# Experts' down product as three rounded products, with the down weights split block by block

## The reference, cut to what matters

```python
gu = jnp.einsum('th,eih->eti', x2, w_gate_up)
g, u = jnp.split(gu, 2, axis=-1)
act = jax.nn.silu(g) * u
out_e = jnp.einsum('eti,ehi->eth', act, w_down)      # the down product
moe_out = jnp.einsum('eth,te->th', out_e, combine)
```

## Time and profile before

| | |
|---|---|
| median of 3 runs | 1449.4 us |
| profiled execution, its own time | 1447.74 us |
| its span | 1445.7 us |
| granted TensorE clock, mean | 0.996 |
| busy share: PE (matmul) / VectorE / ScalarE / GpSimd | 98% / 59% / 35% / 25% |

### The profile page before, as it was taken

How to read it: one execution, slowest core, us unless ns; L and a number is a source line. 1 busy time by engine, 2 the same in 40 slices (tenths; PEclk the granted TensorE clock), 3 DMA queues, 4 the chain that set the end, 5 groups by cost and what they waited for, 6 DMA issues and landing times.

```text
span 1445.7 us, 26892 instructions
## 1 busy us (share of the span) xinstructions
PE 1412.5 (98%) x9085; PEld 1126.2 (78%) x9086; DVE 846.3 (59%) x1804; ACT 512.1 (35%) x1113; POOL 361.5 (25%) x376
## 2 busy tenths in 40 slices
PE   6999997999999999999999999999999999999999
PEld 5888885777878787777878787777877788777777
DVE  5444445666666565666666565666678746243358
ACT  4333343334333333333333333334334330222242
POOL 1222223121111212121121212121112101266746
PEclk9999999999999999999999999999999999999999
DMA  6543431111111111111111101111113243654557
GB/s 223 163 131 123 132 114 43 37 41 37 34 39 38 41 29 49 36 35 37 41 40 31 49 29 41 37 41 37 48 59 102 84 169 132 223 170 161 163 172 276
DMA packets 89882, 125.95 MB, mean 87 GB/s; under 512 B 7120, under 2 KB 56272, under 8 KB 89296
## 3 DMA queue, kind: packets, MB, share of 16 engines
q1 hardware_dynamic: 82288, 100.23, 21.5%
q0 software_dynamic: 7520, 24.65, 5.2%
HBM read 87.36 MB, written 37.49 MB: 86 GB/s over the span
## 4 chain that ended last, share of the span: by engine, by line
PE 93%; DVE 2%; DMA 2%; issue 2%; POOL 1%; ACT 1%; SPq 0%; POOLq 0%; DVEq 0%; ACTq 0%
PE ps L572 23%; PE ps L574 22%; PE ps L573 22%; PE ps L902 5%; PE ps L638 4%; PE ps L680 4%; PE ps L918 3%; PE ps L646 2%; PE ps L665 2%; PE ps L897 1%; PE ps L619 1%; DMA acc<-in_wv 1%; DMA wgu<-in_w_gu 1%; PE ps L816 1%; POOL qr L472 1%
## 5 line engine op out<-in xcount | busy, mean ns | idle before, releaser
L478 POOL CAST vth<-vt 128x256 fp32r<-128x256 f32 x64 | 25.6, 400 | 636.1 <-PE ps L680 636.1
L1069 ACT CAST ah<-ps 128x256 fp32r<-128x256 f32 x256 | 83.5, 382 | 236.4 <-PE ps L574 232.2
L1312 DVE TENSOR_TENSOR acc<-ps,acc 128x512 f32 (+1 forms) x129 | 88.6, 687 | 127.6 <-PE ps L574 127.6
L572 PE MATMUL ps<-hT,w0h 128*128 128x512 f32 (+1 forms) x384 | 154.0, 401 | 0.9 <-DVE w0l L1260 0.9
L574 PE MATMUL ps<-hT,w0h 128*128 128x512 f32 (+1 forms) x384 | 150.6, 392 | 0.0
L573 PE MATMUL ps<-hT,w0l 128*128 128x512 f32 (+1 forms) x384 | 150.1, 391 | 0.0
L472 POOL TENSOR_TENSOR qr<-qv,mhalf 128x8 f32<-128x8 f32 x64 | 105.4, 1648 | 90.2 <-DVE qv L1327 90.2
L1318 DVE TENSOR_TENSOR al<-ps,ah 128x256 fp32r<-128x256 f32 x256 | 95.8, 416 | 50.9 <-ACT ah L1069 50.9
L1036 ACT COPY qs<-ps 128x512 f32<-128x512 f32 x128 | 75.1, 586 | 135.0 <-PE ps L574 131.5
L1045 ACT ACTIVATE pb<-pb 128x256 f32<-128x256 f32 x128 | 48.2, 418 | 175.5 <-DVE pb L1343 175.5
L572 PE MATMUL ps<-w1l,ah 128*128 128x512 f32 x260 | 104.6, 402 | 1.0 <-DVE al L1318 1.0
(11 more groups left out here) (230 smaller groups left out, 3082.5 us busy)
## 6 DMA issues: line engine op xcount, KB each, us to landing
wraw<-in_w_att SPq DMA_DIRECT2D x64, 256.0 KB, 2.6
vbuf<-vo SPq DMA_DIRECT2D x16, 512.0 KB, 3.3
kbuf<-ko SPq DMA_DIRECT2D x16, 512.0 KB, 3.9
kt<-kbuf SPq DMA_DIRECT2D x32, 256.0 KB, 2.9
vt<-vbuf SPq DMA_DIRECT2D x64, 128.0 KB, 2.0
wgu<-in_w_gu SPq DMA_DIRECT2D x4, 2048.0 KB, 8.6
y<-ybuf SPq DMA_DIRECT2D x16, 512.0 KB, 5.7
craw<-in_ctxT SPq DMA_DIRECT2D x9, 512.0 KB, 5.0
```

What stands on the lines that cost most here:

```text
L572: pe.matmul(dst, l_hi, r_lo, start=first, stop=False)
L1069: act.copy(ah[:, bp, :, b2, :], pv_view(bp, b2)).then_inc(a_hi, 1)
L1312: dve.tensor_tensor(dst, PS[6 + bp][:], dst, ALU.add).then_inc(acc_done, 1)
```

## The change

The down product of a block becomes a `split_product`. `acteT` and a new tile `wd` (128 x 512) exist as `h` and `l`, each once. Before each block's down product ScalarE reads the block's expert and rounds that expert's down weights into `wd[0]` after the down product before has ended (`ed_done`); VectorE reads the expert too and writes the rest into `wd[1]`. VectorE writes the activation's rounded part and its rest (two instructions on PS[4] where there was one, the second after the first's semaphore). TensorE no longer reads the expert for the down product, and waits for `wd_lo` as well.

```diff
-            acteT = sb("acteT", [P, P], F32, a)
+            acteT = [sb(f"acteT{'hl'[q]}", [P, P], F32R, a) for q in range(2)]
+            wd = [sb(f"wd{'hl'[q]}", [P, D], F32R, a) for q in range(2)]
...
             def expert_down(b, q):
-                e = expert_of(b)
+                pe.wait_ge(wd_lo, b + 1)
                 pe.wait_ge(eT_evac, b + 1)
                 pe.wait_ge(ye_ok, b + 1)
-                pe.matmul(PS[5 + q][:], acteT[:], wdn[:, bass.ds(e, 1), :].rearrange("p a n -> p (a n)"),
-                          start=True, stop=True).then_inc(ed_done, 1)
+                split_product(pe, PS[5 + q][:], acteT[0][:], acteT[1][:], wd[0][:], wd[1][:], True,
+                              True).then_inc(ed_done, 1)
...
-            pe.wait_ge(wdn_in, 64)
...
-            def act_block(b, q):
+            act.wait_ge(wdn_in, 64)
+            act.wait_ge(slot_ok, 1)
+
+            def round_down(b, first=False):
+                e = act.value_load(ebi[0:1, bass.ds(b, 1)], min_val=0, max_val=E - 1)
+                if not first:
+                    act.wait_ge(ed_done, b)
+                act.copy(wd[0][:], wdn[:, bass.ds(e, 1), :].rearrange("p a n -> p (a n)")).then_inc(wd_hi, 1)
+
+            def act_block(b, q, first=False):
+                round_down(b, first)
                 if not isinstance(b, int) or b + 2 < NB:
...
             act_block(NB - 2, 1)
+            round_down(NB - 1)
...
             def dve_block(b, q, first=False):
+                e = dve.value_load(ebi[0:1, bass.ds(b, 1)], min_val=0, max_val=E - 1)
+                dve.wait_ge(wd_hi, b + 1)
+                dve.tensor_tensor(wd[1][:], wdn[:, bass.ds(e, 1), :].rearrange("p a n -> p (a n)"), wd[0][:],
+                                  ALU.subtract).then_inc(wd_lo, 1)
                 dve.wait_ge(eT_done, b + 1)
-                dve.tensor_copy(acteT[:], PS[4][:, 0:P]).then_inc(eT_evac, 1)
+                dve.tensor_copy(acteT[0][:], PS[4][:, 0:P]).then_inc(eT_hi, 1)
+                dve.wait_ge(eT_hi, b + 1)
+                dve.tensor_tensor(acteT[1][:], PS[4][:, 0:P], acteT[0][:], ALU.subtract).then_inc(eT_evac, 1)
```

More of the change, by code:

```diff
@@ L266, in build @@
         y_scaled = sem("y_scaled")
+        eT_hi, wd_hi, wd_lo = sem("eT_hi"), sem("wd_hi"), sem("wd_lo")
         dve_mark, pool_mark = sem("dve_mark"), sem("pool_mark")
@@ L1219, in act_block @@
                 silu(b + 1, 1 - q)
-            with act.Fori(0, PAIRS) as m:
+            act_block(0, 0, first=True)
+            act_block(1, 1)
+            with act.Fori(1, PAIRS) as m:
                 for q in range(2):
@@ L1672, in dve_block @@
                 dve.tensor_copy(ye[q][:], PS[5 + q][:]).then_inc(ye_ok, 1)
+            dve.wait_ge(slot_ok, 1)
+            dve.wait_ge(wdn_in, 64)
             for b in range(2):
```

## The result

The changed kernel takes 1465.09 us (median of 4 runs, 1463.41 to 1466.12) against 1447.79 (4 runs); ratio 1.0115, 95% interval 1.009 to 1.0139. It is slower by some 17 us. The forecast was 1467, its range 1452 to 1480. The profiled execution of after took 1464.68, its span 1462.9, 17.2 more than before's 1445.7.

What follows compares the result with a forecast made beforehand. TensorE, 98% busy, was taken as the bound, with `acteT` barely in time. 42 intervals at +0.40 (16.8), the last two blocks (+1.9), less 0.6 for loop turns, made +18 on 1447.74: 1465.8, as a median 1467; range 1452 to 1480.

Steps and rivals of the forecast that it cites:

- the ring: Each block: VectorE's queue from `ye` over register read and weights' rest to the activation's rest sets 3.54 us, against 3.14.
- From F to the weights' rest: From a down product's end (F) to the start of VectorE's weights' rest: 1.04 or, with loop branch, 1.29; mean 1.17 us.
- From its end to the weight load: From the activation's rest's end to the down product's first weight load: 0.12 plus 0.05 for another wait, 0.17 us.
- Alternating lengths: Expected sign in the timeline: blocks 3.4 to 3.7 us apart, in two lengths taking turns by about 0.2.
- The stage's sum: Expert stage, 42 block intervals at 0.40 us more each: 16.8, less 0.6 for TensorE's loop turns vanishing in its wait.
- The last two blocks: End of the expert stage, blocks without token transposes: 6.74 us instead of 4.89, so 1.9 more.
- Behind the stage: Code after the expert stage's last down product: nothing changes, 0 us.
- A: Rival: VectorE's register read hides and ScalarE's cast decides; blocks of 3.33 us, +10, 1459 us; chance 0.17.
- B: Rival: the activation's rest is in time and TensorE stays the bound; 2.97 us a block, 1442 us; chance 0.06.
- C: Rival: the activation's two VectorE instructions decide alone, weights' rest being early; 3.20 us a block, 1453 us; chance 0.07.
- D: Rival: VectorE's register read is 0.3 us slower; 3.84 us a block, 1480 us; chance 0.12.
- The two rules: Skill pages weighed against the trace: decoding past a waiting instruction would hide VectorE's read; a 600 ns load floor adds 13 us.

Runs made afterwards that it cites:

- e1: Changed kernel with VectorE's register read (and `gated`) moved ahead of the copy `ye` of the block before; 1453.5 us.
- e2: Changed kernel without the weights' rest and VectorE's register read, the three products using the rounded weights twice; 1449.9 us.
- e5: Changed kernel with two tiles for the rounded weights, so ScalarE's cast waits for the down product of two blocks before; 1466.1 us.
- e4b: e4 with TensorE's register read for the next gate-up moved ahead of the transpose's wait for the activation; 1465.5 us.
- e3: e2 also without the activation's rest, the three products using rounded parts alone; 1442.0 us.
- e8: e7 with the product that takes the weights' rest made last of three, its wait right ahead of it; 1442.9 us.
- e9: e8 with TensorE's step turned round: register read, down product of the block before, token transposes, activation's transpose, gate-up; 1441.4 us.
- e4: Changed kernel with the activation's transpose moved right behind the token transposes, ahead of gate-up and its register read; 1476.4 us.
- e6: Changed kernel with one plain float32 down product on the rounded parts, rests made and waited for but unused; 1469.0 us.
- e7: Changed kernel with e4b's TensorE order and e1's VectorE order, the weights' rest behind the activation's parts; 1445.5 us.
- e10: Kernel before, plain product and no splits, with e9's turned step on TensorE; 1453.1 us.

## Why the prediction was right

**The mechanism** was the one forecast: TensorE idle, 3.516 us a block against 3.54, VectorE's queue behind `ye` the ring that sets it. e1 and e2 show it from both sides: nearly all of the stage's loss goes when the read is moved (12.7 of 14.9 us, with the loop's branch) or left out with the rest it serves, and none when ScalarE's tile is doubled (e5) or the transpose comes earlier (e4b).

**The terms.** From F to the weights' rest 1.17 were put: 1.29 is measured with the branch and 1.24 without. With the branch the sum was exact. Without it the load took 574 ns instead of 354, so the two kinds of block differ by 0.05 there and not by 0.25. The weights' rest to the activation's rounded part 0.61, as put; then 0.32 and 0.29, as put (0.33, 0.29). From its end to the weight load 0.17 were put, 0.07 is measured. The row that gave 0.12 has a wait instruction (line 832, 0.05) running between the release and the load, and 0.05 was added for another. Here TensorE stood in its last wait already, which ended 0.05 after the release, with the load 0.02 behind it. The product 0.97, as put. The two errors, +0.10 and -0.10, cancel; that 3.54 came out so well is partly luck. So is the total, 1467 for 1465.1: the blocks and the stage's end took 2.4 us less than put, and 1.5 came from behind the stage, where nothing was put.

**Alternating lengths** are there early in the stage (3.28 and 3.77), but twice as far apart as forecast and later nearly gone (3.50 and 3.54). Why they die away isn't settled.

**The stage's sum** was put at 16.8 - 0.6 and is 14.1. Blocks of 3.516 instead of 3.54 account for 1.0. The other 1.1 is before's own loss: the 0.04 that its mean block had above 3.14 vanished altogether in TensorE's wait, 1.7 in all, and I had taken off only 0.6. **The last two blocks** took 3.13 and 3.29, put at 3.41 and 3.33.

**Behind the stage** "nothing changes" was wrong, by 1.5 us. All eleven kernels in which ScalarE rounds the weights need 49.9 to 51.4 us there, the three others 48.6. In all eleven the windows view has the lower clock, and in the three 1.00 throughout, from 3 us before F(46) to 10 us behind it. It lasts about 3.4 us in after, e1, e3, e4b, e8 and e9, and about 6.8 in e2, e4, e5, e6 and e7; in e5, e6 and e7 it begins before F(46) and so takes time of the last block too. The code behind F(46) is the same. A longer hole around the last down product would be one reading. It fits after (2.21 and 1.48), but not e3, where TensorE stood for only 0.65 and 1.48, less than the 0.84 and 1.48 of before. Why the clock falls there stays open.

**Rivals.** A supposed that the read hides. It does not in after, but e1 has A's chain: 0.97 until the rest, as A had it (0.96), and 2.26 behind it by the measured terms make 3.23; its longer common block is 3.22. B's gain exists, and needs another order (e7 to e9). C was too dear (e2): with the measured 0.07 in place of 0.17 its sum is 3.10, and 3.10 was measured. D's long loads did come, up to 589 ns, but on half the blocks and not on top of the branch.

**The two rules.** VectorE's branch ran at 1304.7 with `ye`'s start at 1304.69, though it could have been decoded during the 0.54 us in which `ye` waited. Nothing behind the waiting instruction was decoded early. By the Trainium skill's page Perfetto Trace Analysis, section on DVE / Act engine instructions, the sequencer would have been free for the next one; this trace disagrees, as before's did. The loads on VectorE took 302 to 589 ns, median 451. The Trainium skill's page DMA: Bandwidth & Descriptors, under Latency and other measured facts, gives about 600 ns as a floor; all 47 lie below it.

## What to carry to other kernels

A register read or a loop branch is free only while its engine has issued work to run; behind an instruction that waits it is part of the chain, at 0.6 to 1.0 us a read here, and no busy time shows it. So write each engine's step as: reads first, then what is ready, then the wait and what hangs on it; and don't put two reads in a row ahead of an engine's critical product. An engine that is 98% busy can lose its place to one that is 61% busy, so count the ring of waits, not the shares.

## What the runs showed that was not expected

- The same register load on VectorE took 306 ns at the median when it stood ahead of the waits (e1) and 451 behind `ye`, with single ones at 354 and 574. The copy isn't the reason: in e4, where VectorE's order is that of after, the median behind `ye` is 314, and in e6 377. What lengthens the load isn't known.
- A turn of TensorE's loop cost up to 0.08 us before and 0.3 to 0.4 in e1 and e2, 0.2 to 0.3 in e3 and e7: the same instructions, without cover.
- Two reads in a row on TensorE took 1.6 us (1300.55 to 1302.16 in e10), which eight multiplies (1.72 us) do not cover, since the reads begin 0.1 us after the first of them has started, and 0.2 us of waits and register work follow before the down product's load at 1302.43.
- TensorE's clock fell to its lower level around the end of the expert stage in all eleven kernels in which ScalarE rounds the weights, for about 3.4 us in six of them and 6.8 in five. It cost 1.5 us in after.
